# PSUM banks dealt anew in the two attentions of a four-layer float32 block

## The reference, cut to what matters

```
q = (xm @ Wq + bq) / 16;  k = xm @ Wk + bk;  v = xm @ Wv + bv        # layer 0
attn = einsum('bhnd,bhmd->bhnm', q, k) * scale                       # layer 2, after rotary positions
w = softmax(attn, axis=-1)
y = einsum('bhqk,bkhc->bqhc', w, v)
x = x + gate * (y @ Wo + bo)
```

## Time and profile before

| | |
|---|---|
| time, median of 3 runs | 934.22 us (931.71 to 936.51) |
| the profiled execution | 934.88 us, span 932.9 us |
| TensorE busy | 888.0 us, 95% |
| VectorE busy | 589.3 us, 63% |
| ScalarE busy | 521.2 us, 56% |
| first attention's rounds | 69 to 275 us |
| second attention's rounds | 588 to 800 us |

### The profile page before, as it was taken

The page is one execution under the profiler, slowest core; times in us unless marked ns, Lnnn a source line. Parts: engine busy times, 40 slices in busy tenths (PEclk is TensorE's granted clock), DMA queues, the critical chain, the costliest instruction groups (busy, mean ns, idle before and its releaser), DMA issues.

```text
span 932.9 us, 14877 instructions
## 1 busy us (share of the span) xinstructions
PE 888.0 (95%) x5358; PEld 541.1 (58%) x5358; DVE 589.3 (63%) x928; ACT 521.2 (56%) x955; POOL 469.7 (50%) x626
## 2 busy tenths in 40 slices
PE   5999999999999999999999999999999999999997
PEld 3554444443347779677787774344444333687874
DVE  4687887888885465554533287778778895234323
ACT  2226878777775534444464531677867777744331
POOL 4393565655748636446544326658264116664330
PEclk7979999999999999999999999999999999999999
DMA  7565684666213030132223136545545531100001
GB/s 229 149 164 162 164 236 124 179 193 179 73 47 91 1 133 1 47 102 97 97 76 132 14 99 185 176 105 186 165 120 184 147 91 54 37 14 1 23 23 46
DMA packets 67088, 101.32 MB, mean 109 GB/s; under 512 B 19644, under 2 KB 30984, under 8 KB 66632
## 3 DMA queue, kind: packets, MB, share of 16 engines
q1 hardware_dynamic: 58584, 86.90, 31.4%
q0 software_dynamic: 5920, 10.90, 4.6%
q10 hardware_dynamic: 2512, 2.58, 1.0%
HBM read 64.65 MB, written 35.02 MB: 107 GB/s over the span
## 4 chain that ended last, share of the span: by engine, by line
PE 79%; DVE 9%; ACT 4%; issue 4%; POOL 3%; DMA 1%; ACTq 0%; DVEq 0%; POOLq 0%
PE PS L715 13%; PE PS L683 13%; PE PS L1141 12%; PE PS L1123 12%; PE PS L638 5%; PE PS L694 4%; PE PS L621 3%; DVE U L875 3%; PE PS L616 3%; PE PS L454 2%; ACT PH L779 2%; PE PS L651 2%; PE PS L629 1%; PE PS L1259 1%; PE PS L1247 1%
## 5 line engine op out<-in xcount | busy, mean ns | idle before, releaser
L875 DVE TENSOR_REDUCE U<-PS 128x2 f32<-128x1024 f32 x256 | 308.1, 1220 | 60.3 <-PE PS L694 59.0
L779 ACT ACTIVATE PH<-PS 128x512 f32<-128x512 f32 x512 | 277.1, 598 | 94.3 <-PE PS L683 91.3
L683 PE MATMUL PS<-UR 50*128 50x512 f32 x512 | 197.0, 454 | 9.3 <-ACT PH L779 4.7
L694 PE MATMUL PS<-UR 48*128 48x512 f32 x512 | 192.5, 471 | 5.9 <-DVE U L875 5.2
L1189 POOL TENSOR_TENSOR PHR<-PH,PHR 128x512 fp32r<-128x512 f32 x96 | 123.5, 1290 | 117.3 <-ACT PHR L1179 117.3
L683 PEld LDWEIGHTS PS<-UR 50*128 50x128 f32 x512 | 82.6, 186 | 151.2 <-ACT PH L779 84.4
L1141 PE MATMUL PS<-UR,PHR 128*128 128x256 f32 x768 | 158.6, 290 | 2.7 <-POOL PHR L1189 2.5
L715 PE MATMUL PS<-PH,U 128*32 128x512 f32 x1024 | 137.5, 610 | 0.0
L1141 PEld LDWEIGHTS PS<-UR,PHR 128*128 128x128 f32 x768 | 124.6, 189 | 20.1 <-issue 16.0
L1141 PE MATMUL PS<-W2R,PHR 128*128 128x256 f32 x384 | 108.2, 282 | 0.0
L1178 ACT ACTIVATE PH<-PS,col 128x512 f32<-128x512 f32 x64 | 43.9, 687 | 91.8 <-PE PS L1123 91.8
(11 more groups left out here) (256 smaller groups left out, 1387.5 us busy)
## 6 DMA issues: line engine op xcount, KB each, us to landing
UR<-d_parts SPq DMA_DIRECT2D x112, 192.0 KB, 4.2
d_parts<-UR SPq DMA_DIRECT2D x42, 256.0 KB
d_parts<-UR POOLq DMA_DIRECT2D x40, 256.0 KB, 5.4
d_o<-U SPq DMA_DIRECT2D x32, 256.0 KB, 2.5
U<-in_L_cond_W_dram SPq DMA_DIRECT2D x8, 1024.0 KB, 7.5
W<-in_L_cond_W_dram SPq DMA_DIRECT2D x24, 256.0 KB, 3.3
U<-d_o SPq DMA_DIRECT2D x32, 128.0 KB
U<-d_rec SPq DMA_DIRECT2D x16, 256.0 KB
```

Source lines behind the costliest of these rows:

```text
L683: self.close(pe.matmul(dst, KP[g // 2][r:r + SROWS + 2, j, kt * P:(kt + 1) * P], QP[g // 2][r:r + SROWS + 2, j, :], start=True, stop=True) ...
L694: ins = pe.matmul(bank(2 + (w + 2) % 4), QP[g // 2][r:r + SROWS, j, qt * P:(qt + 1) * P], KP[g // 2][r:r + SROWS, j, :], start=True, stop= ...
L779: nc.scalar.activation(PH[:, m % 2, j, :], self.where("ST", n), ACT.Exp).then_inc(self.a_free, 1)
L875: v.tensor_reduce(mx[:, G % 2, :].rearrange("p (r c) -> p r c", r=2)[:, :, c // 2], PS[:, 2 + (w + 1) % 4:4 + (w + 1) % 4, :], AX.X, ALU.m ...
```

## The change

The maxima's scores get three banks, 3 to 5, and every step stands for itself: SM of w waits for the reduction of w - 3, and one VectorE instruction reduces one bank (128 x 512 in, 128 x 1 out). The column of `mx` for each w is the one that it had. ST and the pieces share four banks, 7, 0, 1 and 2, up to step 223 (`TURNS`), and 7, 0, 1 from there to step 260. The MLP's first turn waits in addition for bank 2's last reader.

```
-SHARED = (7, 0, 1)
+SHARED, LAST_SHARED = (7, 0, 1, 2), (7, 0, 1)
+TURNS = 224
...
-            where = early if n < LEAD else SHARED if n <= TAIL else (7, 6)
+            where = early if n < LEAD else SHARED if n < TURNS else LAST_SHARED if n <= TAIL else (7, 6)
...
-                        pe.wait_ge(self.sm_free, 8 * NG)
+                        pe.wait_ge(self.sm_free, 16 * NG)
+                        pe.wait_ge(self.a_free if self.last2[0] == "A" else self.m_free, self.last2[1])
                         self.mlp.turn(pe, 0)
...
                         dst = self.open(pe, kind, b, i)
-                        pe.wait_ge(self.sm_free, 8 * (b + 1))
+                        pe.wait_ge(self.sm_free, 16 * (b + 1))
...
-                        if w % 2 == 0 and w >= 4:
-                            pe.wait_ge(self.sm_free, w // 2 - 1)
-                        ins = pe.matmul(bank(2 + (w + 2) % 4), QP[g // 2][r:r + SROWS, j, qt * P:(qt + 1) * P],
+                        if w >= 3:
+                            pe.wait_ge(self.sm_free, w - 2)
+                        ins = pe.matmul(bank(3 + w % 3), QP[g // 2][r:r + SROWS, j, qt * P:(qt + 1) * P],
                                         KP[g // 2][r:r + SROWS, j, :], start=True, stop=True)
-                        if w % 2:
-                            ins.then_inc(self.sm_full, 1)
+                        ins.then_inc(self.sm_full, 1)
...
-                        where = 2 + (w + 2) % 4 if n < 227 else 4 + w % 2
+                        where = 3 + w % 3 if n < 227 else 4 + w % 2
...
-                    if 0 <= w < NSTEP and w % 2:
-                        u = w // 2
-                        G, c = w // 16, (w - 1) % 16
-                        v.wait_ge(self.sm_full, u + 1)
-                        if u % 8 == 0 and G >= 2:
+                    if 0 <= w < NSTEP:
+                        G, c = w // 16, 8 * (w % 2) + w % 16 // 2
+                        v.wait_ge(self.sm_full, w + 1)
+                        if w % 16 == 0 and G >= 2:
                             self.wait_full(v, "M", G - 2, 0)
-                        v.tensor_reduce(mx[:, G % 2, :].rearrange("p (r c) -> p r c", r=2)[:, :, c // 2],
-                                        PS[:, 2 + (w + 1) % 4:4 + (w + 1) % 4, :],
-                                        AX.X, ALU.max).then_inc(self.sm_free, 1)
+                        v.tensor_reduce(mx[:, G % 2, c:c + 1], bank(3 + w % 3), AX.X, ALU.max).then_inc(self.sm_free, 1)
```

More of the change, by code:

```diff
@@ L162, in slots @@
         for key in keys + ([("ST", n)] if 0 <= n < NSTEP else []):
-            where = early if n < LEAD else SHARED if n <= TAIL else (7, 6)
+            where = early if n < LEAD else SHARED if n < TURNS else LAST_SHARED if n <= TAIL else (7, 6)
             add(key, where[turn % len(where)])
             turn += 1
-    return place, n_act, n_dve, main
+    return place, n_act, n_dve, main, last[2]
 def build(nc, A, out):
@@ L550, in __init__ @@
                 self.norm0 = 0 if a == 0 else 16
-                self.place, self.nA, self.nM, self.nM_main = slots(self.sched, ON_ACT[a], EARLY[a])
+                self.place, self.nA, self.nM, self.nM_main, self.last2 = slots(self.sched, ON_ACT[a], EARLY[a])
             def on_act(self, kind):
@@ L691, in pe @@
                                 pe.wait_ge(first_filled, FILLS)
-                        if w % 2 == 0 and w >= 4:
-                            pe.wait_ge(self.sm_free, w // 2 - 1)
-                        ins = pe.matmul(bank(2 + (w + 2) % 4), QP[g // 2][r:r + SROWS, j, qt * P:(qt + 1) * P],
+                        if w >= 3:
+                            pe.wait_ge(self.sm_free, w - 2)
+                        ins = pe.matmul(bank(3 + w % 3), QP[g // 2][r:r + SROWS, j, qt * P:(qt + 1) * P],
                                         KP[g // 2][r:r + SROWS, j, :], start=True, stop=True)
-                        if w % 2:
-                            ins.then_inc(self.sm_full, 1)
+                        ins.then_inc(self.sm_full, 1)
                     elif NSTEP <= w < NSTEP + LOOK and n < NSTEP:
-                        if w % 2 == 0 and w < NSTEP + 4:
-                            pe.wait_ge(self.sm_free, w // 2 - 1)
-                        where = 2 + (w + 2) % 4 if n < 227 else 4 + w % 2
+                        if w < NSTEP + 3:
+                            pe.wait_ge(self.sm_free, w - 2)
+                        where = 3 + w % 3 if n < 227 else 4 + w % 2
                         r = 64 - 64 * (w % 2)
```

## The result

| | before | after |
|---|---|---|
| median of 4 runs each, same chip | 935.37 us (931.71 to 940.59) | 946.14 us (943.95 to 947.48) |
| the profiled execution, span | 934.88, 932.9 us | 945.51, 943.6 us |
| mean granted clock, profiled execution | 0.984 | 0.984 |
| first PV | 68.93 us | 74.83 us |

A forecast was written before the change was run, and what follows sets the result against it. Three transposed banks for four steps were taken to bound plain rounds; 0.9 - 0.65 - 0.2 + 1.7 + 2.85 + 0.8 = 5.4 us on 934.88 gave 940.3, stated as 940. Forecast's own range 937 to 943, overall 932 to 946.

The forecast's parts named there:

- Plain rounds: Attention rounds without pieces, M or rotation: from 2.61 to 2.72 us, +0.9 us for 8 outside the statistics' groups.
- the round with M: Attention round with M's two VectorE operations and no piece: 3.10 becomes 2.72 us, as M no longer takes ST's turn.
- the next: Round right behind one with M alone: 2.95 instead of 2.71 us; both rounds together -0.13, five times -0.65.
- rounds with pieces: Some 80 rounds from step 34 on, both attentions: TensorE's own work, 3.25 us with Q or K, no wait, cost 0.
- the rival by the Trainium skill's rule: Reductions spaced by their full duration, 0.69 us: plain rounds 2.77, four rounds with one M 11.6, total 946; chance 0.08.
- the group of the statistics: Four rounds around step 212: fourth SM waits behind the statistics, 13.03 for 12.19 us, +1.7 over both attentions.
- Rounds outside the statistics: Attention rounds: plain ones +0.9 us, M alone with the next -0.65, the one behind rotation and M -0.2.
- the first lead: Stretch up to the first PV: rows of four SM wait for the first's reduction, +2.85 us, bounds 1.2 and 4.
- the clock: Rival: more waits in the leads bring more half-level clock, +1.7 us for one lead, +3.4 for both, 942 to 944; chance 0.17.
- the second lead: Stretch between the attentions: M of group 0 and the first ST up to 1.0 us later, +0.8 us (0.3 to 2).

The follow-up runs named there:

- unfilled: Without the fillings, where the changed kernel's TensorE repeats score matmuls while it would wait; fillings measured 945.92 us (step 215), 943.77 us (leads), 943.64 us (both).
- dealt statistics: Statistics of step 212 dealt to steps 177, 181, 185 and 189: 943.58 us on the changed kernel, 935.61 us on the kernel before.
- the experiment with waits on purpose: Changed kernel with statistics dealt to four steps, VectorE reducing one bank four times over at six w in each attention: 979.33 us, ratio 1.0472.

## Why the prediction was wrong, point by point

*Right.* Plain rounds 2.73 (2.72 said), the round with M 2.74 (2.72), the next 2.88 (2.95), rounds with pieces unchanged. Reductions start 0.60 apart, not 0.68, so the rival by the Trainium skill's rule (VectorE: DVE Perf Modes, "The DRAIN you can't avoid") fell (four rounds with one M 11.1, not 11.6). I had read that rule too widely: the same section says that a next operation that is not held starts earlier, and 0.60 for 0.68 fits that. At full clock the group of the statistics is 13.02 to 13.03 in seven instances (13.03 said). Rounds outside the statistics come to -1.1 (with M beside V and T, which I had at nothing), against my +0.05.

*The term that was mis-sized: the first lead.* +2.85 said, +5.9 measured in the first trace. The start up to the Q of 42.99 came 1.84 later (44.83; 0.9 said): w = 6 to 9 are a row of four already, and its fourth SM stands at 44.11, where I had 43.5. Row by row behind it: w = 10 to 13 took 1.14 more (0.45 said), 18 to 21 and 22 to 25 1.0 each (0.5 and 0.8), and from w = 26 to the first PV 8.85 for 7.99, where I had allowed 0.2 because VectorE is the bound there: a whole row of four SM (65.98 to 67.69, 1.71 for 0.76) lies in that stretch. Two mistakes: a row was left out and the one at the start counted in part, and in the rows that ran at half level I took the new wait as partly hidden, though a row costs as much more there (1.14) as at full level (1.0). Over the traces the first PV stands at 68.1 to 70.3 with four banks in the lead (6 versions, median 69.2) and at 71.0 to 77.2 with three, unfilled (8, median 74.5). Part of these 5.3 is half level, of which the second group has more. Traces with as much of it between 38 us and the first PV can be compared: at 6.0 and 6.5 us the first PV is at 70.99 with three banks and 68.07 with four, at 8.0 to 8.8 us it is at 73.18 with three and 68.74 to 69.65 with four. So the bank itself costs 2.9 to 4.4, some 3.6: the upper end of my bounds (4), not their middle.

*The rival that came true beside the forecast: the clock.* I gave it 0.17, for the leads alone, and no place at the statistics, where I had myself put a wait of nearly 2 us: +1.7 said, +5.2 measured in the first trace, 3.5 of it in rounds at half level behind the waits. Of the twelve groups of undealt, unfilled statistics in the traces of three-bank versions (the changed kernel and five experiments), eight fell to half level and took 14.2 to 15.6; of the twelve groups with dealt statistics (two of them in the kernel before) none did. A wait that I price is thus also a chance of the half level behind it: six of twelve in the experiment with waits on purpose. Against this stands the second lead. Between the attentions the ten traces with three banks in the leads have no half level, and four of the six with four banks have some 3.4 us of it. The first round of the second attention takes 3.4 in all ten, and 4.9 or more in four of the six; the -1.6 of the trace compared is that. Fewer waits don't always mean more clock.

*The missing term.* The operation that waits for GpSimd: +0.9. The round takes 4.15 or 4.16 in every trace with three banks there in which the operation stands in it, and 3.24 in all three with four; with the operation and its tile's statistics moved away it takes 3.24 or 3.25. The Trainium skill names such a wait (SBUF — State Buffer, "SBUF: two separate sides"): VectorE in a mode that takes two ports, or with two inputs there, and GpSimd lock a shared pair, each for a whole instruction; the ends, 0.02 us apart, agree. Which mode the operation ran in no trace shows. In the kernel before it lasted 0.41 and four banks hid it, so I read over it.

*Second lead.* +0.8 said, +1.3 measured; M of group 0 and the first ST each come 1.0 to 1.1 later, as said. At full level the stretch between the attentions takes 312.5 and 313.0 with four banks in the lead, and 313.7 to 314.4 with three, unfilled.

With these, 3.6 + 1.3 + 1.7 + 0.9 - 1.1 = 6.4, beside the 5.9 measured at equal clock and the 5.4 forecast. That the forecast is so near is luck in part: the leads were 1.25 and GpSimd 0.9 too small, and the rounds gave 1.15 back that I hadn't counted. Giving the bank back in both leads brought 3.6 at equal clock where the sum has 4.9 for them, so that the terms aren't known to better than a microsecond or so. The rest up to 10.8 goes with the clock, whose own cause from run to run stays open.

## What to carry to other kernels

Count each bank's turns where the matmuls come in a row, not only in the steady rounds: here the bank that moved paid 0.36 in each round with M and cost 0.12 in each plain round and 1.0 in each row of four ahead of the rounds. A wait of TensorE over a microsecond costs its length and, half the time here, one to several us of half-level clock; look at the windows behind it before you price it. Deal a long block on the reducing engine to several steps before you take banks from it, and compare versions at equal mean clock, with a microsecond or two of doubt.

## What the runs showed of the hardware

- A reduction of 128 x 512 from PSUM lasts 0.68 and the next starts 0.60 behind it; one of 128 x 1024 lasts 1.23 with 1.13 between starts.
- 0.01 of mean granted clock goes with 5.5 to 6.1 us of these 935 to 945.
- All operations of L409 and L410 that took more than 0.17 (eight of 24 in either trace, up to 1.28) ran beside a GpSimd instruction and ended 0.02 to 0.03 behind its end.
